# Ten constant matmuls ahead of TensorE's first transposition in a fused two-layer transformer kernel

## The reference, cut to what matters

```python
x = L0_attn_x                                   # 16 batches x 512 tokens x 128, float32
xn = _layernorm(x, axis=-1)
x = x + _L0_attn_ref(xn, ...) + _L0_ffn_ref(xn, ...)   # linear attention; shared + 16 gated experts
xn = _layernorm(x, axis=-1)
x = x + _L1_attn_ref(xn, ...) + _L1_ffn_ref(xn, ...)   # causal softmax attention; best of 8 experts
return x
```

```python
q = jax.nn.relu(jnp.einsum('ble,fe->blf', x, Wq) + bq)
k = jax.nn.relu(jnp.einsum('ble,fe->blf', x, Wk) + bk)
v = jnp.einsum('ble,fe->blf', x, Wv) + bv
kv = jnp.einsum('nld,nlm->ndm', k_, v)
attn = jnp.einsum('nld,ndm->nlm', q_, kv) * z[:, :, None]
probs = jax.nn.softmax(xt @ router_w.T, axis=-1)      # 16 experts, the four best are kept
```

## Time and profile before

| | |
|---|---|
| median of 3 runs | 1286.83 us (1284.19 to 1288.10) |
| the profiled execution | 1289.76 us |
| its span, first to last instruction | 1288.5 us |
| what lies around the span | 1.26 us |
| share of the span: PE, DVE, ACT, POOL busy | 94%, 71%, 71%, 50% |

### The profile page before, as it was taken

The page is one execution under the profiler, slowest core; times in us unless marked ns, Lnnn a source line. Parts: engine busy times, 40 slices in busy tenths (PEclk is TensorE's granted clock), DMA queues, the critical chain, the costliest instruction groups (busy, mean ns, idle before and its releaser), DMA issues.

```text
span 1288.5 us, 28804 instructions
## 1 busy us (share of the span) xinstructions
PE 1215.0 (94%) x10216; PEld 704.0 (55%) x10216; DVE 912.4 (71%) x2442; ACT 915.3 (71%) x1233; POOL 648.0 (50%) x866
## 2 busy tenths in 40 slices
PE   5878999999999999999999999999998888889998
PEld 3334454545454545454454545454534366789998
DVE  5327888888887887888888888787867664345554
ACT  2333787878787878787787878787775657667775
POOL 3451646463646465554646463746462201148885
PEclk8897999999999999999999999999995699999999
DMA  7260506243342516060505153342506310025542
GB/s 243 66 129 21 110 23 148 54 86 78 61 95 45 117 30 128 12 130 21 118 23 116 42 98 75 64 99 41 124 21 203 78 58 14 16 45 61 62 59 26
DMA packets 93236, 97.89 MB, mean 76 GB/s; under 512 B 12840, under 2 KB 73000, under 8 KB 92712
## 3 DMA queue, kind: packets, MB, share of 16 engines
q1 hardware_dynamic: 80248, 86.41, 30.1%
q0 software_dynamic: 12416, 8.99, 5.5%
q10 hardware_dynamic: 432, 0.66, 0.1%
HBM read 69.12 MB, written 26.30 MB: 74 GB/s over the span
## 4 chain that ended last, share of the span: by engine, by line
PE 82%; DVE 6%; issue 4%; ACT 4%; POOL 3%; DMA 1%; ACTq 0%; SPq 0%; DVEq 0%; POOLq 0%
PE PS L632 11%; PE PS L665 10%; PE PS L468 10%; PE PS L516 10%; PE PS L598 6%; PE PS L617 6%; PE PS L676 5%; PE PS L449 4%; PE PS L607 2%; PE PS L482 2%; PE PS L492 2%; PE PS L583 2%; PE PS L460 2%; ACT flow L787 2%; PE PS L540 1%
## 5 line engine op out<-in xcount | busy, mean ns | idle before, releaser
L1224 POOL TENSOR_SCALAR_AFFINE_SELECT flow<-flow 128x256 f32<-128x256 f32 (+1 forms) x448 | 194.3, 448 | 460.0 <-ACT flow L787 456.5
L787 ACT ACTIVATE flow<-PS 128x1024 f32<-128x1024 f32 x320 | 319.0, 1029 | 87.2 <-PE PS L617 86.6
L1045 DVE TENSOR_REDUCE nm<-PS 128x2 f32<-128x1024 f32 x128 | 153.6, 1220 | 65.9 <-PE PS L583 65.6
L632 PE MATMUL PS<-flow 128*32 128x512 f32 (+3 forms) x2048 | 183.9, 455 | 1.8 <-POOL flow L1224 0.8
L516 PE MATMUL PS<-early,down 128*128 128x512 f32 x288 | 156.7, 635 | 6.4 <-POOL early L1211 5.4
L1211 POOL TENSOR_TENSOR early<-early 128x512 f32<-128x512 f32 x128 | 158.4, 1267 | 4.8 <-DMA early<-gate_rows 4.4
L468 PE MATMUL PS<-xnT,up 128*128 128x512 f32 x288 | 151.5, 627 | 4.0 <-DVE at L964 3.8
L778 ACT COPY qp<-PS 2x1024 f16<-2x1024 f16 x128 | 128.5, 1004 | 31.7 <-PE PS L607 29.9
L665 PE MATMUL PS<-xsT,w1s 128*128 128x128 f32 x1152 | 142.5, 277 | 2.2 <-DVE act L1146 2.2
L1248 POOL DMA_INDIRECT out_y<-X,rowu x72 | 112.1, 1556 | 62.2 <-ACT X L831 46.5
L1047 DVE TENSOR_REDUCE nm<-PS 128x2 f32<-128x768 f32 x128 | 121.8, 952 | 26.3 <-PE PS L583 26.1
(11 more groups left out here) (169 smaller groups left out, 2113.8 us busy)
## 6 DMA issues: line engine op xcount, KB each, us to landing
early<-gate_rows SPq DMA_DIRECT2D x128, 256.0 KB, 4.9
qp<-relay_q SPq DMA_DIRECT2D x64, 128.0 KB
kp<-relay_k SPq DMA_DIRECT2D x64, 128.0 KB
xsb<-xs SPq DMA_DIRECT2D x72, 65.0 KB, 1.9
relay_k<-qkh SPq DMA_DIRECT2D x32, 128.0 KB, 2.3
out_y<-X SPq DMA_DIRECT2D x16, 256.0 KB, 2.4
early<-in_w SPq DMA_DIRECT2D x1, 4096.0 KB, 15.6
relay_q<-qkh SPq DMA_DIRECT2D x16, 128.0 KB, 2.3
```

Of the source, the lines that this page charges most:

```text
L632: ins = pe.matmul(m.PS[32 * j:32 * j + 32, m.PV, kt * P:], m.vst[b % 2][:, kt, 4 * g + j, :], m.pt[:, r, k * L + o:k * L + o + L - kt * P] ...
L787: act.activation(m.pt[:, n % RING, :], m.PS[:, i:i + 2, :].rearrange("p k c -> p (k c)"), ACT.Exp, scale=1.0 / SCALE).then_inc(s["exp"], 1)
L1045: dve.tensor_reduce(nm[:, 3, 2 * n:2 * n + 2], ps, AX_X, ALU.max, negate=True).then_inc(s["max"], 1)
L1224: ins = pool.affine_select(part, part, [[0, part.shape[1]], [1, P]], ALU.is_ge, nothing, base=0, channel_multiplier=-1)
```

## The change

TensorE no longer waits first for d_first. It waits for "begun", multiplies the constant tile neghalf (128 rows, 4 columns, as the stationary operand) with 512 columns that all are neghalf's first column, ten times, into 4 partitions of PSUM bank 7, and only then waits for d_first and walks the order as before. Nobody reads the ten results. Bank 7 is first used after that by the second kvr matmul, on the same engine. No other engine's list changes, and no semaphore is added.

```diff
+AHEAD = 10
...
+    pe.wait_ge(s["begun"], 1)
+    half = m.neghalf[:, 0:1].to_broadcast([P, L])
+    for _ in range(AHEAD):
+        pe.matmul(m.PS[0:NT, 7, :], m.neghalf[:, :], half, start=True, stop=True)
     pe.wait_ge(s["d_first"], 16 * 3)
```

## The result

| | kernel before | changed kernel |
|---|---|---|
| runs | 19 | 19 |
| median | 1288.10 us | 1291.66 us |
| lowest to highest | 1284.09 to 1292.33 | 1287.91 to 1294.63 |
| ratio | | 1.0022, 95% interval 1.0011 to 1.0032 |
| profiled execution | 1289.76 (span 1288.5) | 1288.95 (span 1287.5) |

The change costs 0.22%, some 2.8 us, against a forecast of 0.21%; the interval reaches from 1.4 to 4.1 us, so that the two agree to 0.01% is luck. The profiled execution of the changed kernel is 0.8 us shorter than that of the kernel before; it lies near the low end of its runs. The whole spans of two executions say nothing at this size. The first 50 us do, and what happens between 60 and 121 us tells why the rest doesn't.

The account below looks back on a forecast made before the run. The prediction took TensorE, 82% of the chain, as the bound, with a first-batch relay between engines. 3.7 us overrun less 0.44 less 0.62 gave +2.7: 1286.8 + 2.7 = 1289.5 us, range 1286.5 to 1297.5.

Parts of the forecast that it names:

- The overrun: Start of TensorE's list: ten matmuls, 20 passes, end at 12.0 against rows ready for 8.33, 3.7 us late.
- What comes back: First batch at full clock: transpositions up to ScalarE's copy gain 0.44 us, first L460 pair up to L902 gains 0.62.
- VectorE as the bound of the first product: After the first L902, VectorE needs 0.91 us per quarter, so the remaining L460 and L475 passes gain nothing.
- The stall as a term of zero: VectorE's L916 waits through L1188, L1189 and the fills, released where it was before relative to L902: zero.
- The half clock before attn0: TensorE idles about 6 us before attn0, the clock falls again and the warm-up is lost there: term zero.
- The carry: From L916 to 47 us and into later batches, the 2.7 us delay goes through unchanged.
- how it would be seen: Signs in the changed kernel's timeline, among them the third batch and those after it late by the same 2.7 us.
- the clock doesn't rise under the constant passes: Rival: TensorE's 20 passes stay at half clock, transpositions come 10.0 us late, 1296.8 us; chance 0.15.
- second witness: Against the unraised clock: at 29.5 it rose just after L500's four transpositions, with 16 stationary columns and 128 rows.
- slip in front of GpSimd: Rival: L916 comes ahead of L1188, attn0 starts 2.7 us earlier at full clock, some 5 us gained, 1281.5; chance 0.05.

Follow-up runs that it names:

- the later fills: GpSimd waits for the first batch's kvm before filling; ratio to the kernel before 0.9982 without constant matmuls, 1.0000 with ten, 0.9984 with six.
- fillx0: Kernel before, no constant matmuls, GpSimd's fills waiting for kvm and batches 2 to 15 of x loaded behind the gates' transfers: 0.9953, 1281.08 us.

## Why the prediction was right

- **The overrun.** Forecast: transpositions at 12.0, ends 11.5 and 12.7. Measured 11.53 in the changed kernel's profile, 12.81 in its second one, 0.1 beyond the upper end, and 12.21 with the later fills. In the first the clock rose 3.4 us after TensorE started, the lower end of the bounds; in the second about 6.0, as worked out from the distances of its weight loads. Passes took 0.854 and 0.431 as priced, with 4 columns as with 128.
- **What comes back.** 0.44 and 0.62 us forecast. From the first transposition to the first L902 passed 3.08 us before and 2.10 in the changed kernel: 0.98 for 1.06. The lateness at the first L902 was 2.22 for 2.7, nearly all of that difference being the clock's early rise. Counted from the rows' readiness in its own execution (9.29) TensorE overran by only 2.2 us, so this one pair of profiles doesn't give the price by itself. Over the profiles with ten full constant matmuls the first L902 comes at 13.63, 14.90 and 14.31, over those without any at 11.41, 11.72, 11.50 and 11.45: 2.8 us later on the mean. (The terms of the forecast sum to 2.64, which it rounds up to 2.7.)
- **VectorE as the bound of the first product.** This holds: 0.88 us a quarter, with TensorE delivering each 0.46. The prediction had 0.91 and so missed that VectorE would gain 0.3 us on the way to L1188 (+1.91 there). Before, its quarters had come at TensorE's pace, and its own is a little faster.
- **The stall as a term of zero.** This holds in the trace (L921 from within L1193 to the end of the fills), and the later fills show its cause. The Trainium skill, "SBUF — State Buffer", section on the two sides, says that GpSimd and an operation of VectorE that uses both its ports exclude each other for a whole instruction. The 6.37 us under fills and the 1.10 us under L1189 agree. The same section of the Trainium skill gives the shared ports to whichever starts first; that agrees as well in fillx0, where L916 started 0.05 us behind L1189 and took 1.07. That L916 is an operation that uses both ports no run shows directly. The trace shows one thing more: L921 did not end at any of the four borders between GpSimd's five instructions that followed one another without a pause (19.6 to 25.9), and in the kernels with later fills it ended with L1194 or L1189, behind which GpSimd paused for 0.43 us.
- **The half clock before attn0.** TensorE rested from 20.2 to 26.08, and attn0 ran at 0.50 from 25.1 on, as forecast (in the kernel before from 22.8 on). All that had been warmed up was lost there.
- **The carry.** Six matmuls cost nothing that shows, ten cost 2.6 and 2.8 us, twenty 9.7, and ten on 32 rows, at half clock, 9.9, against 2.2 to 3.5, 10.5 and 10.0 us at the first L902. The delay goes through, within intervals of 1.4 to 3.4 us to either side. Six on 32 rows don't fit as well: 0.9 us (at most 3.1) against 3.2 at the first L902. Why is open. What the prediction said on how it would be seen was wrong: the later batches did not stand 2.7 us late in the profile but 0.95 early, since stretches at half clock between 60 and 121 us fell otherwise. The argument held for the mean of the runs, not for one execution.
- **The rivals.** That the clock doesn't rise under the constant passes was a real possibility: with 4 columns and 128 rows it rose, with 4 columns and 32 rows it didn't, and the price was then 9.9 us (6.5 to 13.3) for the 10.0 of the prediction. The prediction's second witness is weak: L500 was not alone before the rise at 29.5, since L492's sixteen passes had kept TensorE busy for 4.2 of the 5.3 us, so that row can't tell what transpositions do. L916 did not slip in front of GpSimd: it came 1.03 us behind the start of L1188's counterpart, worked out as 0.83.

## What to carry to other kernels

Warming TensorE in a wait is free only as long as it ends before the wait does, since an in-order engine can't drop the rest; size the passes at the slow rate, and ask which engine bounds the work that is to run warm. Here VectorE did, from the first product on, so 6 us at half clock were worth 1. The same 25 us held 6 us of gain elsewhere: one-time fills on GpSimd that held up a small operation of VectorE on the path, and a large load that stood in the way of a small transfer. The load's move alone brought nothing, the fills' move alone some 2 us (at most 5), and both together 6.

## What the runs showed of the hardware

- With passes of 4 stationary columns over 128 rows TensorE's clock rose between 2.8 and 6.0 us after they began (seven profiles, worked out from the distances of the weight loads; 3.4 in the changed kernel's). The same passes over 32 rows stayed 0.854 us apart for all 17.1 us. Whether this has to do with the stretch of the earlier trace rows that stayed at 0.50 is not shown: its largest group worked on 128 rows.
- The clock fell again within the relay of the first batch, at 11.5 us, in the profile of six constant matmuls and later fills: behind the constant passes TensorE paused for 1.15 us, made four transpositions and paused for 0.68. In the profile of six without later fills, with pauses of 0.50 and 0.67 us, it did not fall there. A head start that ends on time may thus be lost before it is used.
- A VectorE operation on 16 columns that takes 0.23 us by itself took 1.07 to 1.16 where it started early in a two-input operation of GpSimd, and 5.2 to 6.4 beside a row of GpSimd instructions without pauses.
- A transfer of 32 KB that landed in 2.2 us with the queues empty took 6.7 (22.66 to 29.34) behind a load of 3.7 MB issued before it.
